# A fused layer-norm, scan and FP4 kernel: a bank for group 0, big numbers by ScalarE, scaling and adding on GpSimd, zero matmuls early, new orders

## What is computed

```
xn  = layernorm(x)                                   # x: (4, 1024, 128)
out = x + scan(xn) + ffn(xn)
scan: y_t = Re(gate * (sum_s phazor^(t-s) * init * xn_s  +  last * phazor^(t+1)))   # per channel
ffn:  q(w) = FP4 (E2M1) quantised and dequantised, in blocks of 16 along the last dimension
      h   = silu(q(xn) @ q(w_gate).T) * (q(xn) @ q(w_up).T)      # 352 hidden columns
      ffn = q(h) @ q(w_down).T
```

## Time and profile before

| | before |
|---|---|
| median of 3 runs | 132.06 us (132.04 to 132.09) |
| the profiled execution's span | 131.0 us |
| PE busy | 114.4 us, 87% |
| DVE busy | 106.0 us, 81% |
| POOL busy | 102.4 us, 78% |
| ACT busy | 100.8 us, 77% |

### The profile page before, as it was taken

How to read it: one execution, slowest core, us unless ns; L and a number is a source line. 1 busy time by engine, 2 the same in 40 slices (tenths; PEclk the granted TensorE clock), 3 DMA queues, 4 the chain that set the end, 5 groups by cost and what they waited for, 6 DMA issues and landing times. The chain is left out here.

```text
span 131.0 us, 2333 instructions
## 1 busy us (share of the span) xinstructions
PE 114.4 (87%) x657; PEld 86.2 (66%) x657; DVE 106.0 (81%) x217; ACT 100.8 (77%) x198; POOL 102.4 (78%) x145
## 2 busy tenths in 40 slices
PE   3800799999949999999999999999799999999992
PEld 3700355446528777757777887777586888788792
DVE  0867949898699879999879998987699899998610
ACT  4287563998858699997799979876959797939840
POOL 4698998699999989999999998994978499630000
PEclk9985555999995999999999999999999999999999
DMA  3990000000000000002001100200020020020202
GB/s 120 323 343 31 3 0 3 0 3 0 0 0 5 0 0 0 0 9 76 0 0 43 39 5 3 80 0 0 0 80 5 0 80 0 0 85 0 83 0 80
DMA packets 3323, 4.90 MB, mean 37 GB/s; under 512 B 496, under 2 KB 1392, under 8 KB 3312
## 3 DMA queue, kind: packets, MB, share of 16 engines
q1 hardware_dynamic: 3168, 4.77, 10.6%
q10 hardware_dynamic: 144, 0.00, 0.1%
HBM read 2.67 MB, written 2.10 MB: 36 GB/s over the span
## 5 line engine op out<-in xcount | busy, mean ns | idle before, releaser
L1140 PE MATMUL ps_u<-wu_T,xq_T 128*128 128x352 f32 x64 | 24.5, 492 | 2.6 <-DVE hq L1590 2.6
L1125 PE MATMUL ps_g<-wg_T,xq_T 128*128 128x352 f32 x64 | 26.0, 489 | 0.1
L1191 PEld LDWEIGHTS ps_o<-wd_T,hq_T 128*128 128x128 f32 x174 | 23.1, 200 | 2.5 <-issue 0.7
L1191 PE MATMUL ps_o<-wd_T,hq_T 128*128 128x128 f32 x174 | 24.4, 285 | 0.0
L807 ACT COPY hq_T<-ps_h 128x384 f32<-128x384 f32 x32 | 15.2, 474 | 6.9 <-PE ps_h L1159 6.8
L801 ACT ACTIVATE silu<-ps_g 128x352 f32<-128x352 f32 x32 | 14.8, 463 | 3.3 <-PE ps_g L1125 2.9
L1590 DVE TENSOR_TENSOR hq<-ps_u,den 128x704 f32<-128x704 f32 (+1 forms) x17 | 14.2, 833 | 2.7 <-PE ps_u L1147 2.7
L1159 PE MATMUL ps_h<-ident,hq 128*128 128x128 f32 x96 | 16.2, 279 | 0.1
L1140 PEld LDWEIGHTS ps_u<-wu_T,xq_T 128*128 128x128 f32 x64 | 11.4, 200 | 7.1 <-DVE hq L1590 3.1
L1159 PEld LDWEIGHTS ps_h<-ident,hq 128*128 128x128 f32 x96 | 12.1, 145 | 5.1 <-issue 3.4
L1545 DVE TENSOR_TENSOR ps_u<-silu,ps_u 128x704 f32<-128x704 f32 (+1 forms) x17 | 14.3, 841 | 1.4 <-PE ps_u L1140 0.8
(11 more groups left out here) (166 smaller groups left out, 248.8 us busy)
## 6 DMA issues: line engine op xcount, KB each, us to landing
x_all<-x_in SPq DMA_DIRECT2D x8, 256.0 KB, 5.1
out<-x_all SPq DMA_DIRECT2D x7, 256.0 KB, 2.0
w_raw<-w_in SPq DMA_DIRECT2D x2, 192.0 KB, 3.9
out<-x_all SPq DMA_DIRECT2D x4, 64.0 KB, 1.6
w_raw<-w_in SPq DMA_DIRECT2D x1, 176.0 KB, 3.9
par<-params_in ACTq DMA_DIRECT2D x1, 3.5 KB, 3.0
```

Source lines behind the costliest of these rows:

```text
L1125: pe.matmul(ps_g[:, 0:I], x_cols(t), wg_T[:, :], start=True, stop=True).then_inc(s_gate, 1)
L1140: pe.matmul(slot(q)[:, j, 0:I], x_cols(t), wu_T[:, :], start=True, stop=True).then_inc(s_up, 1)
L1191: m = pe.matmul(out_cols(t), hq_T[t % NHT][:, c * P:(c + 1) * P], wd_T[:, c, :], start=False, stop=(c == NCH - 1), skip_group_check=True)
```

## The change

- **Group 0 is rounded in a bank.** `divide_x(0, n)` and `scale_x(0, n)` go to DVE, with the half of x in `ps_x` (n = 0) or `ps_o` (n = 1), and PE rounds it there with two matmuls of 256 columns (`round_x`). `centre` goes to ACT.
- **Normalising.** ACT now normalises groups 0 to 3, GpSimd groups 4 to 7.
- **Four pairs of h (4, 6, 8, 10)** are scaled on GpSimd. ACT first copies the rounded slot to `codes` (bf16), which frees the slot; then GpSimd multiplies with the scales (`scale_codes`).
- **Parts of y.** For groups 4 to 7 GpSimd adds y_im to y_re (`add_y`), and PE transposes one tensor in place of two.
- **x in the last banks** is put there by ACT (`open_last`), not by PE.
- **The transpose of xn** writes the bank with every fourth column, so that the copy `copy_xnT` on ACT has both sides contiguous.
- **Zero matmuls.** 34 matmuls on an operand of zeros stand between the first steps of PE, in place of 16 transposes of the identity. The constants that were columns are immediates now.
- **Orders.** All lists are written in another order.

```diff
+    IN_BANK = (0,)
+    XN_ACT = (0, 1, 2, 3)
+    BY_POOL = (4, 6, 8, 10)
+    BIG_DVE = ()
+    X_OPEN = True
+    NC = 2
+    Y_POOL = (4, 5, 6, 7)
...
+            def scale_codes(q):
+                pool.wait_ge(s_code, sum(1 for k in BY_POOL if k <= q))
+                pool.wait_ge(s_den, q + 1)
+                if q >= NH:
+                    pool.wait_ge(s_hT, PAIR * (q - NH + 1))
+                c = codes[BY_POOL.index(q) % NC].rearrange("p j (b e) -> p j b e", e=BLK)
+                pool.tensor_tensor(hq_blocks(q), c, pair_scales(den[q % ND]), ALU.mult).then_inc(s_hqp, 1)
...
+            def add_y(g):
+                pool.wait_ge(s_yre, g + 1)
+                pool.wait_ge(s_yim, g + 1)
+                pool.tensor_tensor(y_re[g % NY][:, :], y_re[g % NY][:, :], y_im[g % NY][:, :],
+                                   ALU.add).then_inc(s_yap, 1)
...
-                act.copy(in_tiles(xn_T[g % NU]), ps_x[:, :].rearrange("d (j p) -> d j p", j=TG)).then_inc(s_xnTc, 1)
+                act.copy(xn_T[g % NU][:, :], ps_x[:, :]).then_inc(s_xnTc, 1)
...
+            def copy_codes(q):
+                act.wait_ge(s_hr, q + 1)
+                if BY_POOL.index(q) >= NC:
+                    act.wait_ge(s_hqp, BY_POOL.index(q) - NC + 1)
+                act.copy(codes[BY_POOL.index(q) % NC][:, :, :], in_slot(q)).then_inc(s_code, 1)
...
+            def stay_busy(n):
+                pe.wait_ge(s_idle, 1)
+                for _ in range(n):
+                    pe.matmul(ps_h[:, :], idle[:, 0:P], idle[:, :], start=True, stop=True)
...
-                    m = pe.transpose(ps_x[:, j * P:(j + 1) * P], xn[g][:, j * D:(j + 1) * D], ident[:, :])
+                    m = pe.matmul(in_tiles(ps_x)[:, j, :], xn[g][:, j * D:(j + 1) * D], ident[:, :],
+                                  start=(j == 0), stop=(j == TG - 1), is_transpose=True, skip_group_check=True)
...
+            def round_x(g, n):
+                pe.wait_ge(s_xbig, x_big(g, n))
+                pe.wait_ge(s_unit, 2)
+                b = xbig[g % NXB][:, xcols(g, n)]
+                pe.matmul(quarter(g, n), unit[0][:, :], b, start=False, stop=False, skip_group_check=True)
+                pe.matmul(quarter(g, n), unit[1][:, :], b, start=False, stop=True,
+                          skip_group_check=True).then_inc(s_pr, 1)
```

More of the change, by code:

```diff
@@ L128, in build @@
         hq = [sb(f"hq{k}", [P, PAIR, I]) for k in range(NH)]
+        codes = [sb(f"codes{k}", [P, PAIR, I], BF16) for k in range(NC)]
         hq_T = [sb(f"hq_T{k}", [P, NCH * P]) for k in range(NHT)]
@@ L251, in build @@
         first_re, first_im, neg_turn = col(18), col(19), col(20)
-        base_c, quarter_c, round_c, unround_c = (consts[:, n:n + 1] for n in range(4))
         DECAY_STEPS = 18
@@ L607, in _ @@
             normalise(5, 3)
-            shift_x(4, 1)
-            shift_back_x(4, 1)
-            scale_x(4, 1)
+            divide_x(2)
+            demodulate_re(0)
+            demodulate_im(0)
+            shift_x(2)
+            shift_back_x(2)
+            scale_x(2)
+            divide_x(3)
+            modulate_re(0)
+            modulate_im(0)
+            shift_x(3)
+            shift_back_x(3)
+            scale_x(3)
+            demodulate_im(1)
+            divide_x(4)
+            normalise(6, 0)
@@ L665, in load_silu @@
             def load_silu():
-                act.activation(silu[0][:, 0, 0:1], p(V_LND), ACT.Silu)
+                act.activation(col(21), p(V_LND), ACT.Silu)
             def unit_matrix(k):
@@ L850, in _ @@
+            big_x(0, 0)
+            big_x(0, 1)
+            normalise(1, 0)
+            normalise(1, 1)
+            copy_weight(0)
+            big_down()
+            copy_xqT(0, 0)
+            normalise(1, 2)
+            copy_weight(1)
+            copy_xqT(0, 1)
+            silu_tile(0)
+            normalise(1, 3)
+            normalise(0, 0)
+            normalise(0, 1)
+            silu_tile(1)
+            normalise(0, 2)
+            normalise(0, 3)
+            sine()
             diagonal(0)
@@ L894, in _ @@
+            normalise(3, 2)
+            copy_xnT(0)
+            normalise(3, 3)
+            silu_tile(5)
+            copy_in_table(1)
             square_x(2, 1)
             big_x(2, 1)
-            silu_tile(7)
-            copy_hT(1)
-            open_out(0)
-            out_table(0)
-            copy_hT(2)
-            square_h(2)
+            copy_hT(0)
+            open_out(0)
+            silu_tile(6)
+            copy_hT(1)
+            square_h(2)
+            copy_hT(2)
+            big_h(2)
@@ L1638, in _ @@
             moments(7)
+            first_totals()
             weight_maxima(0)
@@ L1734, in _ @@
             inverses_x(2)
+            scale_h(1)
+            maxima_x(3)
             product(2)
-            maxima_x(3)
             maxima_h(2)
-            scale_h(1)
             scales(2)
```

1005 lines of the change are left out of this document (549 added, 456 removed).

## The result

| | before | changed |
|---|---|---|
| median | 132.07 us (132.04 to 132.09, 4 runs) | 121.98 us (121.87 to 122.09, 4 runs) |
| ratio | | 0.9225, 95% interval 0.919 to 0.926 |
| the profiled execution's span | 131.0 us | 119.9 us |

The kernel became 10.1 us faster, where the prediction had 5.7 us and ended its range at 123.8.

What follows compares the result with a forecast made beforehand. PE was taken as the bound in the last two thirds, DVE next. Span 131.0 - 2.6 - 1.7 - 1.6 + 0.7 - 0.5 = 125.3 us, so 126.4 us of time (chance 0.43); range 123.8 to 129.8 us.

Steps and rivals of the forecast that it cites:

- what lies around the span: Time outside the profiled span, 1.06 us, added to each predicted span to get the time.
- PE's own work: Where PE is the bound, 16 y_im transposes and three identity matmuls fewer take 2.6 us off the path.
- start, to the end of tile 7's up matmul: Up to the up matmuls of tiles 6 and 7, new lists remove a 1.89 us wait: gain 1.7 us.
- the second fall of the clock: At 39.3 to 42.6 us PE's half speed should go, as its long pause goes: gain 1.6 us.
- wait for xq of group 4: Near 60 us PE waits for GpSimd, which has more work by then: charge 0.7 us.
- tail: Behind group 6's last `sum_down`, two roundings and two `turn_h` cover ACT's waits: gain 0.5 us.
- the slower rival: GpSimd's last addition ends the chain late, so the kernel is slower: 132.6 us, chance 0.07.
- The one with the full clock from the start: Zero matmuls keep PE's clock full from the start, 1.6 us less: 124.8 us, chance 0.25.
- The gain is taken back: From 43.83 us, time taken from PE returns as waits for `scale_h`, no tail gain: 128.8 us, chance 0.12.
- The strided transposes: Transposes of xn into every fourth bank column cost 3.1 us more in all: 129.5 us, chance 0.11.
- T3: Theory made after the result: work taken from GpSimd and DVE removed PE's waits; no size given.
- T4: Theory made after the result: the new orders removed PE's waits; no size given.

Runs made afterwards that it cites:

- e3: Changed kernel, but PE again transposes both parts of y of groups 4 to 7 and GpSimd adds none: 123.55 us.
- e9: Kernel before without the 16 transposes of y_im of groups 4 to 7, nothing put in their place: 131.88 us, against 132.67 beside it.
- e11: Kernel before with one more matmul ahead of `turn_h` for tiles 8 to 29, 3.6 us of PE's work: 133.65 us, against 132.67 beside it.
- e13: Kernel before with DVE's scaling of pairs 4, 6, 8 and 10 cut to one block, 2.9 us less: 132.87 us, against 132.3 beside it.
- e16: Kernel before with three quarters of GpSimd's `shift_back_x` of groups 2 to 7 left out, 5.1 us less: 130.13 us, against 132.3 beside it.
- e2: Kernel before with 50 zero matmuls in its start in place of 16 transposes of the identity: 132.23 us, against 132.39 beside it.
- e15: Changed kernel with the twelve tiles of groups 1 to 3 normalised on GpSimd again instead of ACT: 124.93 us.
- e1: Changed kernel without any of its zero matmuls: 122.20 us.
- e7: Kernel before, own orders, with GpSimd adding y of groups 4 to 7 and ACT opening the last banks, 2.6 us off PE: 132.79 us.
- e5: Kernel before with `scale_h(1)` moved early in DVE's list, right behind `inverses_x(2)`: 132.14 us, against 132.23 beside it.

## Why the prediction was wrong in size

**Direction and the kinds of step were right, the size was half.** Against 130.0 us, the span that belongs to the times, the gain is 10.1 us.

| step of the prediction | forecast | found |
|---|---|---|
| what lies around the span | 1.06 us | 2.0 us |
| PE's own work | -2.6 | -2.6, and worth it only with the other changes (of 1.9 us e3 costs nearly all, e9 gives a quarter) |
| start, to the end of tile 7's up matmul | -1.7 | -3.6 |
| the second fall of the clock | -1.6 | -1.0 in the profile, 0 in the times |
| wait for xq of group 4 | +0.7 | 0 |
| tail | -0.5 | -0.1 |
| waits of PE between tile 7 and the tail | 0 | -3.8 (what is left of 10.1; 2.4 of it shows as idle time) |

- **What bounds the kernel** is the step that failed most. "Only less work on PE, or fewer of its short waits, makes that stage shorter" is half wrong: by e9, e11, e13 and e16 the pace came from GpSimd through xq and xn, and less work on PE, 98% busy by the profile, mostly made its waits longer. I looked for PE's waits in the views as they stood, 1.72 of 84.87 us idle, and took them for what there was to gain. A count by the prices of the prediction shows more. From the end of tile 7's up matmul to the last matmul PE has 82.1 us of rows at their packed prices in e2 and takes 88.5, of which 2.9 are idle; in the changed kernel it has 81.4 and takes 83.8, 0.5 idle. So by this estimate its waits fell from 6.4 to 2.4 us, and more than half of those 6.4 counted as busy.
- **GpSimd was charged where it should have been credited.** The prediction summed its 89.6 us of work from 26.5 us on and feared its lateness (+0.7, and the slower rival). The 5.4 us of normalising taken from it counted nowhere; e15 puts them at 3.1 us, with 5.8 us less on ACT. It ended its list ahead of 112 us, where the sum had 116.1.
- **The start.** The first gate matmul without zero matmuls came at 16.59 us (e1), by the walk 16.9. But `product(0)` came at 18.34 us, and in e1 at 19.56, where the walk had 21.5: it kept PE at half rate to 21 us, as before, and in e1 the matmuls are at the full rate by 16.6. The walk's late transposes of xq of group 1 (30.1 us) follow from that; they stand at 27.75. Against e2, whose clock is full, tile 7's up matmul ends 5.4 us earlier (39.27 and 33.84, by the start of the next row), less 1.8 us of work that PE hadn't yet done: 3.6 us. How much of this the bank for group 0 brings, and how much the orders, was not run; the zero matmuls bring 0.3 to 0.5 (e1).
- **The clock.** The rule "half the time at half speed comes back" was applied to a stretch in which PE waits for others anyway. The first fall gives nothing (e2), the second 1.0 us.
- **The rivals.** The one with the full clock from the start was right on the clock (all slices 9) and wrong on its worth. "The gain is taken back" is what happens in the old orders (e7, e9), and not with the new lists and loads. The strided transposes were at no cost: 273 ns in both layouts, and 0.44 us for four. The Trainium skill, page Advanced Engine Details and Errata, section PSUM Cachelines, says that any non-contiguous pattern slows matmuls significantly; for transposing matmuls of f32 into every fourth column, the measurement decides against it. GpSimd ending the chain didn't come: it stood idle 1.5 us of 78, not 10 of 93.
- **Small prices held.** Scaling codes 1.38 us (taken 1.6), an addition 1.28 (1.27), the contiguous copy 0.58 (0.59). DVE's 256 columns cost 0.42, not 0.30, and a tile normalised on ACT 0.49, not 0.447. ACT's faster big numbers of h (17 x 0.085 = 1.4 us) weren't in the sum.
- **Slips that entered no term.** At 0.87/0.62 the 11.5 us would grow by 4.6 us, more than the slack of 3.8 that it was said to be within; the additions cost 1.28 us and the scalings 1.38, so it didn't happen. The 0.64 us for a zero matmul at the half clock came from a row's length (0.48 us), where matmuls of the same 384 columns begin 0.27 to 0.32 us apart (13.72, 13.99 and 14.31 us in the profile of before). The lower end of the range takes 1 us off for a charge of 0.7.

How the 3.8 us of waits share out among orders and moved loads can't be told as a sum: undone one at a time in the changed kernel, the scalings are worth up to 5.2 us, the normalising 3.1, the early `scale_h(1)` 2.9, ACT's copy 2.0 and PE's work 1.9, together more than the whole gain. So T3 and T4 both hold in part. Two of the steps were tried in the kernel before and brought nothing there without the rest (e5, e7). What the new lists alone bring, with the old loads, was not run.

## What to carry to other kernels

A busy share of 98% on one engine doesn't make it the bound, all the more where its rows overlap, so that short waits count as busy: leave 2 us of its work out, with nothing in its place, and see whether they come off. Do the same to each of the others, since the engine that sets the pace may be the third by share and show only as a wait of 1 us of somebody else. And sum against the span of the executions that the times are of, not against that of the one that was profiled.
